# Attention and routed FFN: phi, relu and exp moved up inside a period, 1e-6 added by ScalarE's copy

## What is computed

```
xn = layernorm(x)
q, k, v = split(xn @ w_attn.T);  phi(a) = elu(a) + 1
per chunk of 128 tokens, per head:
    scores = mask(phi(q) phi(k)^T)
    num = scores v + phi(q) S;   den = scores.sum(-1) + phi(q) z
    S += phi(k)^T v;             z += phi(k).sum
y = num / (den + 1e-6);  x1 = y @ w_proj.T
e = argmax(xn @ gate_w.T + gate_b + expert_bias)
out = x + x1 + relu(xn @ w1[e] + b1[e]) @ w2[e] + b2[e]
```

## Time and profile before

| what | us |
|---|---|
| median of 3 runs (517.59 to 517.72) | 517.67 |
| the profiled execution's own time | 517.73 |
| its span | 515.9 |
| TensorE busy | 463.5 (90%) |
| VectorE busy | 405.0 (78%) |
| ScalarE busy | 279.2 (54%) |
| GpSimd busy | 259.7 (50%) |

### The profile page before, as it was taken

One profiled execution on the slowest core, in us unless ns is written; L12 is line 12 of the kernel. 1 busy time (PEld: TensorE's weight loads), 2 busy tenths in 40 slices (PEclk: granted clock), 3 DMA queues, 4 the chain that ended last, 5 costly groups with the idle time before them and its releaser, 6 DMA issues.

```text
span 515.9 us, 17895 instructions
## 1 busy us (share of the span) xinstructions
PE 463.5 (90%) x6291; PEld 376.1 (73%) x6291; DVE 405.0 (78%) x881; ACT 279.2 (54%) x537; POOL 259.7 (50%) x468
## 2 busy tenths in 40 slices
PE   1789898998989989889976599999999999999996
PEld 0668776777767778678754488888888888888884
DVE  3788998989989899898877367777777776776775
ACT  3448777787777887777965033323323323333331
POOL 4345667767667676676655424244334333333222
PEclk9799999999999999999998589999999999999999
DMA  8525555575565645655531522222212212210000
GB/s 254 204 65 172 170 183 165 176 226 166 175 179 173 214 171 171 183 180 181 170 124 61 172 67 73 64 78 74 69 53 67 82 55 78 72 50 28 22 17 1
DMA packets 34452, 62.98 MB, mean 122 GB/s; under 512 B 5694, under 2 KB 10175, under 8 KB 34241
## 3 DMA queue, kind: packets, MB, share of 16 engines
q1 hardware_dynamic: 29376, 49.24, 30.0%
q0 software_dynamic: 4992, 12.60, 8.1%
HBM read 51.06 MB, written 13.50 MB: 125 GB/s over the span
## 4 chain that ended last, share of the span: by engine, by line
PE 55%; DVE 24%; issue 9%; POOL 6%; ACT 4%; DMA 1%; DVEq 0%; POOLq 0%; ACTq 0%
PE ps L621 21%; PE ps L634 20%; DVE AR L729 5%; DVE MX L769 4%; DVE AR L723 2%; DVE AR L673 2%; PE ps L492 2%; PE ps L590 2%; POOL W L1279 2%; DVE st L660 2%; PE ps L445 1%; PE ps L507 1%; PE ps L393 1%; PE ps L461 1%; PE ps L418 1%
## 5 line engine op out<-in xcount | busy, mean ns | idle before, releaser
L621 PEld LDWEIGHTS ps<-AR,W 128*128 x1872 | 132.2, 99 | 39.8 <-issue 1.1
L621 PE MATMUL ps<-AR,W 128*128 128x128 f16 x1872 | 156.3, 221 | 0.9 <-ACT AR L1183 0.9
L634 PE MATMUL ps<-W,ST 128*128 x624 | 150.4, 326 | 0.0
L1192 ACT ACTIVATE ST<-ST 128x512 f16<-128x512 f32 x78 | 49.2, 631 | 116.3 <-DVE ST L1018 116.3
L1341 POOL DMA_INDIRECT out<-AR x39 | 39.6, 1016 | 118.5 <-DVE AR L1050 116.4
L1018 DVE SCALAR_TENSOR_TENSOR ST<-ps,TAs,B1S 128x512 f32<-128x512 f32 x78 | 58.6, 751 | 48.6 <-PE ps L621 48.6
L1279 POOL TENSOR_TENSOR W<-ST,W 128x512 f16<-128x512 f32 x64 | 74.2, 1160 | 25.5 <-ACT W L1135 25.0
L729 DVE TENSOR_TENSOR AR<-ps,CT 128x512 f32<-128x512 f32 x128 | 81.9, 682 | 3.6 <-PE ps L435 3.5
L1030 DVE SCALAR_TENSOR_TENSOR ST<-ST 128x512 f16<-128x512 f32 x78 | 53.6, 687 | 15.6 <-ACT ST L1192 15.6
L1336 POOL DMA_INDIRECT AR<-scr,AR x39 | 40.2, 1032 | 31.0 <-issue 21.6
L393 PE MATMUL ps<-xT,WA 128*128 128x128 f16 x768 | 50.8, 225 | 4.0 <-DVE WA L699 2.2
(11 more groups left out here) (144 smaller groups left out, 715.9 us busy)
## 6 DMA issues: line engine op xcount, KB each, us to landing
ST<-in_w SPq DMA_DIRECT2D x128, 256.0 KB, 4.1
scr<-XR SPq DMA_DIRECT2D x32, 256.0 KB, 2.1
XR<-in_x SPq DMA_DIRECT2D x32, 128.0 KB, 4.5
AR<-in_b SPq DMA_DIRECT2D x1, 1024.0 KB, 5.2
AR<-in_wall SPq DMA_DIRECT2D x2, 388.0 KB, 3.9
AR<-scr,AR POOLq DMA_INDIRECT x39, 3.4
out<-AR POOLq DMA_INDIRECT x39, 2.5
ST<-in_cst SPq DMA_DIRECT2D x1, 576.0 KB, 4.0
```

Of the source, the lines that this page charges most:

```text
L621: a = e.matmul(dst, W[:, off:off + 57472][:, bass.ds(place_of(s), 128)], XT16[s % 2][:, xl * 256 + k * 128:xl * 256 + (k + 1) * 128], star ...
L634: a = e.matmul(PS[4 + s % 2][:, 0:w], src[h % 4][:, fs], W[:, off:off + 57344 + w][:, bass.ds(place_of(s), w)], start=(f == 0 and w == 512 ...
L1192: e.activation(HH[h % 4], H32[h % 2], ACT.Relu).then_inc(a_hh, 1)
```

## The change

On VectorE `phi` of the newest chunk, p - 1 instead of p - 2, stands behind `nb(p)` and `route(p)` and in front of `res(p - 4)`, in the period in which its exp is made; before, it opened the next period. The first `w_max` moves from in front of `route` to behind `na`, next to the second. In `y` the addition of 1e-6 is gone and the reciprocal reads PSUM.

On ScalarE both instructions for the first weight quarter stand behind `xTc`, `relu` and `exp` come right behind `y2`, `xh` behind them, and the second quarter (in periods from 32 on, the second and third) comes last. `y1` adds a bias by partition, 1e-6 on each partition that holds a denominator and 0 elsewhere, from a new column of the constants. In period 0 `xh` stays ahead of the weights' rounding.

```diff
-C_ID, ..., C_T, C_N = (..., 274 + 10 * NP, 275 + 10 * NP)
+C_ID, ..., C_T, C_EP, C_N = (..., 274 + 10 * NP, 275 + 10 * NP, 276 + 10 * NP)
...
-                e.tensor_scalar(d, o[:, :, 16:17], 1e-6, None, ALU.add).then_inc(dv.up(), 1)
-                e.wait_ge(dv.sem, dv.n)
-                e.reciprocal(DN[:, :], DN[:, :]).then_inc(dv.up(), 1)
+                e.reciprocal(d, o[:, :, 16:17]).then_inc(dv.up(), 1)
...
             for p in range(NC + 3):
-                if on(p - 2):
-                    phi(p - 2)
...
                 if on(p) and p > 0:
                     nb(p)
-                w_max(2 * p)
+                route(p)
+                if on(p - 1):
+                    phi(p - 1)
                 if p == 2:
                     exponent_b1()
-                route(p)
...
                     na(p + 2)
+                w_max(2 * p)
                 w_max(2 * p + 1)
...
-                e.activation(YT1, PS[5][:, :], ACT.Copy).then_inc(S["y1"], 1)
+                e.activation(YT1, PS[5][:, :], ACT.Identity, bias=cc(C_EP, 1)).then_inc(S["y1"], 1)
...
                 q = list(new_quarters(p))
                 for n in q[:1]:
                     w_scale(n)
-                if on(p - 2):
-                    kt(p - 2)
...
                     w_hi(n)
-                for n in q[1:]:
-                    w_scale(n)
-                    w_hi(n)
                 if on(p - 4):
                     y2(p - 4)
-                if on(p):
-                    xh(p)
...
                 if on(p - 1):
                     relu(p - 1)
                     exp(p - 1)
+                if on(p) and p > 0:
+                    xh(p)
+                for n in q[1:]:
+                    w_scale(n)
+                    w_hi(n)
...
+    cst[:, C_EP] = np.where(i % 32 == 16, 1e-6, 0.0)
```

## The result

| | before | changed |
|---|---|---|
| median, us | 517.69 | 533.84 (532.23 to 535.32) |
| ratio | 1 | 1.0303 (95% interval 1.0266 to 1.0340) |
| profiled execution, span | 517.73, 515.9 | 534.17, 532.3 |
| TensorE busy | 463.5 (90%) | 466.1 (88%) |
| VectorE busy | 405.0 (78%) | 405.4 (76%) |

The kernel is 16.2 us slower: the forecast had 9.6, and its range ended at 532. The direction was right, and in the steady stretch the mechanism and the time too; the size of the whole was not. Busy times hardly changed; what was added is waiting.

What follows compares the result with a forecast made beforehand. The order of work was taken to bound the kernel, as a closed ring of operations on VectorE. Steady stretch +10.3, start +1.1, end -1.6, period 31 -0.2: +9.6 on 517.73, forecast 527.3 us, range 518 to 532.

Steps and rivals of the forecast that it cites:

- The odd period: First stage: phi waits 0.70 us for exp, starts 5.18 behind the first masks; 2.66 more make the period 7.84.
- The even period: First stage: GpSimd's chain and nb's collision with w_lo make a pair of periods 16.58 us instead of 15.95, before routing.
- the 0.2 for routing: Estimated addition per pair, for a routing operation between nb and phi in some even periods, no longer covered.
- The clock in the steady stretch: TensorE's granted clock in the first stage's steady stretch, 1.00 before, was expected to hold.
- the rival of a falling clock: TensorE at 1.2 GHz for qk in each even period: 20 us more, 547; chance 0.03.
- The addition: The 1e-6 addition in y, 0.21 us a period: alone worth 5.5 us, in the new order nothing.
- from there on VectorE waits for nothing: Kernel before, plain odd period: once y starts, 1.99 us behind the first masks, VectorE has no further wait.
- The start: Periods before 5: xh(1) behind relu and exp delays nb(2) by 1.4; +1.1 us at period 5, between 0 and 1.4.
- The end: Last periods: fewer weight quarters in front of y2, and no addition: -1.6 us, between 0 and -2.2.
- y2's wait in periods 32 and 33: ScalarE's weight quarters delayed y2, so pr waited; gains of 0.6 us in period 32 and 0.4 in 33.
- Sum: Whole kernel: 10.3 + 1.1 - 1.6 - 0.2 = +9.6 us on 517.73, so 527.3.
- a ring: Closed loop of first-stage operations, from mask 0 to the next mask 0, setting the period: 7.97 us before.

Runs made afterwards that it cites:

- e2_scalar: Kernel before with only ScalarE's new order (and period 1's moved weight rounding), VectorE in the old order: 536.83 us, ratio 1.0342.
- e6_quarter: Changed kernel with the second weight quarter's w_scale and w_hi back in front of y2 in periods under 32: 532.04 us, ratio 1.0262.
- e7_start: Changed kernel with the old order of VectorE and ScalarE in periods 0 to 4: 531.66 us, ratio 1.0244.
- e11_xh: Changed kernel with xh back in front of relu and exp in periods 1 to 4 alone: 537.57 us, ratio 1.0403.
- e12_wm_start: Changed kernel with the first w_max and the exponents back in front of phi in periods 0 to 4 alone: 533.00 us, ratio 1.0304.
- e13_stat: Changed kernel with the statistics of chunk p + 2 in front of phi in periods 1 to 4 alone: 532.61 us, ratio 1.0277.
- e5_nn_first: Changed kernel with GpSimd's nn_end in front of km in even periods: 531.43 us, ratio 1.0264.
- e14_xh_stat: Changed kernel with xh in front of relu and exp and the statistics in front of phi, in periods 1 to 4 alone: 533.99 us, ratio 1.0286.
- e1_add: Kernel before with only the edit of y and y1 (no addition, reciprocal from PSUM, bias on y1): 515.18 us, ratio 0.9943.
- e9_best: Kernel before with the edit of y and y1 and GpSimd's nn_end in front of km: 513.67 us, ratio 0.9934.
- e10_nn_only: Kernel before with GpSimd's nn_end in front of km and nothing else: 516.59 us, ratio 0.9982.

## Why the prediction failed, step by step

- **The odd period: right.** 7.84 forecast, 7.82 measured (8.02 where the largest weight's steps are). phi starts 5.16 to 5.18 behind the first masks in every odd period, behind a wait of up to 0.60.
- **The even period: right.** 16.58 a pair and 0.2 for routing, so 16.78; measured 217.57 / 13 = 16.74. e2_scalar shows that this chain alone is enough for it; e6_quarter, that the second quarter's `w_hi` is one link of it, worth 3.2. That the total agrees to 0.1 us is luck in part: the even periods lie between 8.53 and 9.13, around the forecast's 8.94, the 0.2 for routing was an estimate, and in three of them another operation was held than nb.
- **The clock in the steady stretch: right.** 1.00 from period 5 to 31; the rival of a falling clock didn't occur there. At both ends TensorE runs at half speed in part, in the kernel before too, and the forecast had no term for a change of that.
- **The addition: mis-sized.** In the new order it is worth nothing, as forecast. "Alone it would give 26 x 0.21 = 5.5 us" was wrong: it gave 2.85, since "from there on VectorE waits for nothing" held only until it was 0.1 faster; then pr decided in odd periods, and w_lo, which holds nb, in even ones with routing.
- **The start: wrong by its mechanism.** "+1.1, between 0 and 1.4" had xh as the only cause, and said that phi(1), free of xh(2), would give some back. nb(2) was 1.4 later, as worked out. But the phi that then waits has work behind it which VectorE formerly did while ScalarE was busy: exponents, statistics, w_max, masks. And the statistics feed the root. The order's part is 2.9 to 3.7 us, where 1.1 was forecast. Shown by e7_start (all of it back), e11_xh (xh alone gives nothing back), e12_wm_start (w_max and the exponents, 1.7 at period 3) and e13_stat (the statistics' place is the largest part: 40.94 instead of 42.6 to 42.7, at the same speed of these scores).
- **The end: wrong sign.** "-1.6, between 0 and -2.2" came from y2's wait in periods 32 and 33. Period 32 gave 0.58 of it (8.54 to 7.96; forecast 0.6 and 0.21), and pr has no wait there, as forecast. Period 31 took 0.10 more, where 0.2 less was forecast. Period 33 gave 9.92 instead of 9.17: the quarters that were moved out of y2's way run as w_lo beside three routing operations, whose rows above are 0.59, 0.75 and 0.95 us longer. This cost has no term in the forecast. Two executions with the changed kernel's instructions and order in these periods show what one of the three is worth. In e5_nn_first and e14_xh_stat (rows above) L913 met no w_lo and took 1.27 instead of 2.22, and period 33 took 8.97 and 8.94 instead of 9.92, although TensorE was slower there. From period 34 to the gather come 1.71 more, with the clock at 0.64 instead of 0.80.
- **Sum.** The spans differ by 16.4, the forecast had 9.6. Of the 6.8 between them 2.6 lie at the start (3.73 for 1.1), 3.8 from period 31 to the gather (+1.98 for -1.8) and 0.4 behind the gather, where the forecast had nothing.

**What stays open.** Why TensorE's granted clock is so different from period 34 on. With the old order at the end the stretch from period 34 to the gather took 15.63 us at 0.99 (e1_add), 15.73 at 0.81 (e9_best), 15.76 at 0.85 (e10_nn_only) and 16.12 at 0.80 (before). With the changed kernel's instructions and order there it took 16.59 at 0.85 (e5_nn_first), 17.40 at 0.75 (e14_xh_stat), 17.83 at 0.64 (changed), 18.00 at 0.69 (e13_stat), 18.97 at 0.56 (e11_xh), 18.98 at 0.55 (e12_wm_start) and 19.90 at 0.50 (e7_start). So the clock differs between executions with the same order, and no run shows a step that sets it. From period 31 to the gather these seven took 41.1 to 45.4 us, 43.4 on average, and the four with the old order 40.0 to 41.3, 40.7 on average. The +1.98 of the end is thus a size of one execution, no constant of the change; the sign is borne out by the averages. Of period 33's collisions the one of L913 is shown to cost about 0.95; what the two smaller ones cost alone no run separates.

## What to carry to other kernels

When an instruction that waits is moved forward in a stream, price all that now stands behind it, in the ramp as well as in the steady loop: in the ramp nothing else fills the wait, and a small operation behind it (here the statistics) may feed the chain that it waits for. Work that is moved out of one operation's way on ScalarE comes out later on GpSimd; look up which VectorE instructions then run beside it. And a saving on a ring is worth only what the next limit leaves: here res was 0.1 us from TensorE's pr.

## What the runs showed of the hardware

- Small VectorE operations beside GpSimd's w_lo or km lose as much as large ones: L839 took 0.82 instead of 0.23, the cast L849 0.96 instead of 0.21, the scan L855 1.25 instead of 0.31, L717 (8 columns) 0.96 instead of 0.17, nb 1.23 instead of 0.40. From 40 to 262 us res (L760, 0.41 or 0.42) and w_max (L767, 1.24 to 1.26 for two) are never longer: res has one input in PSUM, w_max has a single input. The Trainium skill (SBUF — State Buffer, Who interferes with whom) says that a VectorE instruction with two SBUF inputs contends with a GpSimd instruction that reads SBUF, that casts and tensor_scalar can, and that whoever is first holds the pair. The trace agrees. The scan isn't named there, but its two inputs are in SBUF, and it was held as the rule for two SBUF inputs has it. For the order it agrees in direction: behind w_lo nb lost 0.83, and ahead of it (e9_best) 0.05, with 0.05 lost by w_lo.
- A chain of tiny GpSimd operations is dear: the 14 of nn_begin and nn_end work on 128x2 elements, last 0.19 to 0.22 us each at steps of 0.28, and take with km nearly 5 us between two w_lo. They set the pair in the new order.
- The first and last periods vary by 1 to 3 us between executions whose instructions and order there are the same: period 5 opened at 42.59 to 44.01, and the stretch from period 34 to the gather took 16.59 us at a granted clock of 0.85 and 19.90 at 0.50. The kernel before varies too: its runs beside the experiments lay between 515.11 us, at a mean granted clock of 0.981, and 522.90 at 0.965. A forecast that sums those periods from a single profile carries that error.
